# A graph layer on one core: ScalarE and SyncE wait on the gathers' own semaphores, GpSimd waits once per group, and the lists are gathered in 124, 122, 125 and 77 rows

## The reference

```
xp    = xn @ W                                   # 4 heads of 64
e     = leaky_relu(a_src[src] + a_dst[dst], 0.2)
alpha = exp(e - segment_max(e)) / segment_sum(exp(e - segment_max(e)))
gat   = relu(segment_sum(alpha * xp[src], dst))
mix   = (v + l2norm_over_channels(q2) @ (l2norm_over_nodes(k2).T @ v) / sqrt(N)) @ W_out + b_out
x     = x + gat + mix
x     = x + sum over 8 experts of w_e * (two normed hidden layers of 256 and an output layer)(layernorm(x))
```

## Time and profile before

| what | value |
|---|---|
| median of 3 runs | 4459.44 us (4455.92 to 4459.45) |
| span of the profiled execution, first to last instruction | 3169.3 us |
| own time of the profiled execution apart from its span | not given in its page |
| median less that span | 1290.1 us |
| mean granted TensorE clock | 0.893 |
| PE busy | 2799.6 us, 88% |
| DVE busy | 2292.7 us, 72% |
| ACT busy | 1531.0 us, 48% |
| POOL busy | 1491.4 us, 47% |
| gathers of L755 | 1564 |

### The profile page before, as it was taken

One profiled execution on the slowest core, in us unless ns is written; L12 is line 12 of the kernel. 1 busy time (PEld: TensorE's weight loads), 2 busy tenths in 40 slices (PEclk: granted clock), 3 DMA queues, 4 the chain that ended last, 5 costly groups with the idle time before them and its releaser, 6 DMA issues. The chain is left out here.

```text
span 3169.3 us, 61855 instructions
## 1 busy us (share of the span) xinstructions
PE 2799.6 (88%) x18584; PEld 2138.8 (67%) x18584; DVE 2292.7 (72%) x6615; ACT 1531.0 (48%) x4018; POOL 1491.4 (47%) x1580
## 2 busy tenths in 40 slices
PE   7777787888788998889888888879999999999999
PEld 6566676666667877777766777766666666666665
DVE  7587787878788787877888888885766665656633
ACT  3354465555555666656655655653333333333332
POOL 0777777777777777777777777720000000000000
PEclk9787787888778898889887887889999999999999
DMA  9544444444445555555544444433011010101000
GB/s 307 147 120 124 121 126 121 124 122 128 118 117 132 138 141 135 141 135 136 131 124 129 122 125 124 125 99 111 10 38 36 12 35 12 35 12 35 12 12 12
DMA packets 208686, 315.91 MB, mean 100 GB/s; under 512 B 84449, under 2 KB 142818, under 8 KB 208226
## 3 DMA queue, kind: packets, MB, share of 16 engines
q0 software_dynamic: 75360, 212.42, 25.9%
q1 hardware_dynamic: 125250, 92.39, 9.7%
q10 hardware_dynamic: 7744, 7.15, 0.7%
HBM read 279.46 MB, written 26.86 MB: 97 GB/s over the span
## 5 line engine op out<-in xcount | busy, mean ns | idle before, releaser
L755 POOL DMA_INDIRECT xg<-edge_table,idx x1564 | 1486.2, 950 | 523.0 <-issue 491.4
L1059 PE MATMUL ps_y<-y,hotw 128*128 128x260 f32 x3512 | 859.0, 407 | 69.9 <-issue 68.0
L1059 PEld LDWEIGHTS ps_y<-y,hotw 128*128 128x128 f32 x3512 | 689.9, 203 | 217.2 <-issue 81.6
L1809 DVE SCALAR_TENSOR_TENSOR xg<-ps_ye,wts,xg 128x256 f32<-128x256 f32 x392 | 189.7, 484 | 401.6 <-PE ps_ye L1599 401.4
L911 ACT ACTIVATE y<-xg,w 128x65 f32 x1756 | 463.3, 337 | 7.1
L1291 DVE TENSOR_TENSOR y<-xg,ps_v 128x780 f32<-128x780 f32 x439 | 417.0, 960 | 8.9 <-DVE ps_v L1284 0.5
L1642 ACT ACTIVATE tables<-ps_h,bnb,bns 128x448 f32<-128x448 f32 x224 | 162.3, 724 | 494.2 <-PE ps_h L1589 494.2
L970 ACT CAST hotw<-hot 128x512 f32<-128x512 bf16 x439 | 266.5, 622 | 246.4 <-PE ps_y L1059 246.0
L1599 PE MATMUL ps_ye<-wo,xg 128*128 128x256 f32 x1568 | 354.2, 383 | 0.2 <-DVE xg L1809 0.2
L1589 PE MATMUL ps_h<-xg,w 128*128 128x448 f32 x896 | 347.5, 541 | 1.0 <-issue 0.5
L1589 PE MATMUL ps_h<-tables,w 128*128 128x448 f32 x896 | 345.9, 539 | 0.0
(11 more groups left out here) (283 smaller groups left out, 3155.6 us busy)
## 6 DMA issues: line engine op xcount, KB each, us to landing
xg<-edge_table,idx POOLq DMA_INDIRECT x1564
mix_rows<-kk SPq DMA_DIRECT2D x49, 257.0 KB
xg<-mix_rows SPq DMA_DIRECT2D x7, 1799.0 KB, 8.4
xb<-in_xt SPq DMA_DIRECT2D x50, 128.0 KB
xnk<-in_x SPq DMA_DIRECT2D x50, 128.0 KB
x<-in_x SPq DMA_DIRECT2D x7, 896.0 KB, 11.4
xt<-in_xt SPq DMA_DIRECT2D x7, 896.0 KB, 13.4
xb<-in_xt SPq DMA_DIRECT2D x24, 256.0 KB
```

Of the source, the lines that this page charges most:

```text
L755: pool.indirect_dma_start(xg[:, q * OCT + u, j, :], None, dr["table"], bass.IndirectOffsetOnAxis(ap=idx[o % IDX][:, c:c + 1], axis=0)).the ...
L1059: mm = pe.matmul(ps_y[v % 2][:, 0:RW], hotw[v % 2][:, j, :], y[v % 2][:, j, :], start=(j == 0), stop=(j == CH - 1))
L1809: dve.scalar_tensor_tensor(yb[q][:, j, :], ps_y[j % 2][:, 0:D], wts[q][:, j, e:e + 1], yb[q][:, j, :], ALU.mult, ALU.add).then_inc(S["expe ...
```

## The change

Three things change.

The semaphore `landed` is gone. ACT and SP wait on `got[0]` and `got[1]` themselves. The count for each is made by `words` for both parities, so `K.need` becomes two tables, with three DVE operations each in place of one, and ACT reads four values per step in place of two.

GpSimd no longer waits ahead of a group's fourth gather for the group before. It waits ahead of a group's first gather for the last group but one, which is the last with the same semaphore.

The four list gathers take 124, 122, 125 and 77 rows (`LIST`, starting at `LAT`), and all that handles the lists follows.

```diff
-VT = NVT // P + 1
+LIST = (124, 122, 125, 77)
+LAT = (0, 124, 246, 371)
+VT = len(LIST)
...
-        rows = [min(P, NVT - t * P) for t in range(VT)]
+        rows = LIST
...
                 def words():
-                    link(dve.tensor_scalar(K.need[:], grp[0:1, :], 1.0, float(ONE), ALU.add, ALU.add))
+                    for k in range(2):
+                        link(dve.tensor_scalar(slot_i[:], grp[0:1, :], 2.0 - k, None, ALU.add))
+                        link(dve.tensor_scalar(slot_i[:], slot_i[:], 1, None, ALU.arith_shift_right))
+                        link(dve.tensor_scalar(K.need[k][:], slot_i[:], 1.0, 16.0 * CH, ALU.max, ALU.mult))
...
+                        if not first or u >= 2:
+                            pool.wait_ge(got[u % 2], 16 * CH * ((o * OCT + u) // 2))
                         for j in range(CH):
-                            if j == CH - 1 and not (first and u == 0):
-                                pool.wait_ge(got[(u - 1) % 2], o * (16 * CH * OCT // 2) + 16 * CH * ((u - 1) // 2 + 1))
-                                pool.sem_inc(landed, 1)
                             c = u * CH + j
...
-                    sp.wait_ge(landed, ONE + (o - IDX + 1) * OCT)
+                    for k in range(2):
+                        sp.wait_ge(got[k], 16 * CH * (o - IDX + 1) * OCT // 2)
...
-                        need.append(act.value_load(K.need[0:1, bass.ds(n(SV) + v, 1)], min_val=ONE + 1, max_val=ONE + NGP))
+                        need.append([act.value_load(K.need[k][0:1, bass.ds(n(SV) + v, 1)], min_val=16 * CH, max_val=16 * CH * NGP) for k in range(2)])
...
-                            act.wait_ge(landed, need[v > 0])
+                            for k in range(2):
+                                act.wait_ge(got[k], need[v > 0][k])
```

More of the change, by code:

```diff
@@ L234, in _ @@
                             sp.wait_ge(rows_in[t], 16)
-                            sp.dma_start(dr["dst"][t * P:t * P + rows[t], :], xrows[0:rows[t], t, 0:GE]).then_inc(stored, 16)
+                            sp.dma_start(dr["dst"][LAT[t]:LAT[t] + rows[t], :], xrows[0:rows[t], t, 0:GE]).then_inc(stored, 16)
                 for k in range(IDX):
@@ L288, in turn_groups @@
                     for t in range(VT):
-                        pe.transpose(ps_g[0:rows[t], t * P:(t + 1) * P], grp[:, t * P:t * P + rows[t]], ident).then_inc(gt_d, 1)
+                        pe.transpose(ps_g[0:rows[t], t * P:(t + 1) * P], grp[:, LAT[t]:LAT[t] + rows[t]], ident).then_inc(gt_d, 1)
                 def turn_lists(t):
@@ L386, in lists_out @@
                     act.wait_ge(last_t, t + 1)
-                    act.copy(K.last[:, t * GE:t * GE + r * CH].rearrange("p (v j) -> p j v", j=CH),
+                    act.copy(K.last[:, LAT[t] * CH:LAT[t] * CH + r * CH].rearrange("p (v j) -> p j v", j=CH),
                              ps_l[:, 0:GE].rearrange("p (j v) -> p j v", j=CH)[:, :, 0:r]).then_inc(lastc_d, 1)
@@ L510, in spreads @@
                     r = rows[t]
-                    at = slice(t * GE, t * GE + r * CH)
+                    at = slice(LAT[t] * CH, LAT[t] * CH + r * CH)
                     dve.wait_ge(rel_t, t + 1)
@@ L514, in spreads @@
                                       ps_r[:].rearrange("p (j v) -> p j v", j=CH)[:, :, 0:r],
-                                      bc(base[:, t * P:t * P + r], 1, CH), ALU.subtract).then_inc(rel_d, 1)
+                                      bc(base[:, LAT[t]:LAT[t] + r], 1, CH), ALU.subtract).then_inc(rel_d, 1)
                 def centre(i):
@@ L619 @@
     score_capped weights_done values_copied q_turned q_squared q_fourth mix_products mix_copied hot_widened y_done_act max_joined tail_first tail_second
-    tail_third pair_parts max_shifted max_leaky y_done y_summed acc_scaled acc_done asrc_packed iota_set weights_spread fold_spread groups_landed
+    tail_third pair_parts max_shifted max_leaky y_done y_summed acc_scaled acc_done asrc_packed iota_set weights_spread fold_spread
     k_products k_biased k_squared k_less k_scales k_normed k_sums_done k_sums_added k_columns_added one_set k_rooted kv_products kv_done root_bounded
@@ L684, in attend @@
          vo_d, qt_d, q2_d, q4_d, mix_d, mixc_d, hotw_d, ya_d, msum_d, tp1_d, tp2_d, tp3_d, pp_d, z1_d, lk1_d,
-         y_d, py_d, sc_d, acc_d, as_d, iota_d, wv_d, fov_d, landed,
+         y_d, py_d, sc_d, acc_d, as_d, iota_d, wv_d, fov_d,
          k_d, kb_d, k2_d, kr1_d, kr_d, kn_d, ka_d, kas_d, col_d, one_d, root_d, kv_d, kvs_d, lim_d, rec_d, kv1_d,
@@ L759, in _ @@
                     octet(o % 2, o, o == 0)
-                pool.wait_ge(got[(NG - 1) % 2], 16 * CH * ((NG + 1) // 2))
-                pool.sem_inc(landed, 1)
+                for k in range(2):
+                    pool.wait_ge(got[k], 16 * CH * ((NG + 1 - k) // 2))
                 for c in K.exp.values():
@@ L1848, in graph_layer @@
             K.blk, K.slot = ml.sb("blk", [1, NVT // 4], I32), ml.sb("slot", [1, NVT // 4], I32)
-            K.need = ml.sb("need", [1, NVT], I32)
+            K.need = [ml.sb(f"need{k}", [1, NVT], I32) for k in range(2)]
             K.freed = ml.sb("freed", [1, NGP // PACE], I32)
```

## The result

The changed kernel takes 4475.86 us (median of 20 runs, 4463.61 to 4491.41), the kernel before on the same chip 4459.52 us (20 runs, 4445.55 to 4480.04). The ratio is 1.0033, with a 95% interval of 1.0021 to 1.0046: slower by 16.3 us between the medians and by 15 us by the ratio, where the forecast was 6.4 us faster. 4475.86 lies outside the range of 4438 to 4467.

A forecast was written before the change was run, and what follows sets the result against it. GpSimd's pace of one gather every 1.25 us was taken to bound the edge loop up to about 1680 us, the consumer after. Terms -10 + 2.0 + 1.6 = -6.4 us gave 4459.4 - 6.4 = 4453.0 us, range 4438 to 4467.

The forecast's parts named there:

- The lists: In `prepare`, ahead of the edge loop: uneven list gathers lengthen the transfers by 1.6 us, with 0 and 3.3 as ends.
- by the rule the sum would be 1.7 us higher: List gathers: if the largest divisor up to 16 sets the engines (4, 2, 5, 11), the sum rises 1.7 us.
- `words`: +2.0 us: Ahead of `rstd(6)`: five more DVE operations delay the last rows, barrier and first gather by 2.0 us, in full.
- The moved wait: -10 us: GpSimd in the edge loop: waiting at a group's first gather saves 10 us on the path, bounds 8 and 11.
- the direct waits: ACT and SP waiting on the DMA semaphores themselves: 0 us, with -2 us as the bound.
- The tail: End of the edge loop: last gather near 2076 us, the last step's copies 10 to 14 us after it.
- More value loads: 0: ACT, two more loads per step: hidden behind queued products and a wait for PE, 0 us, upper bound +3 us.
- neither rival on them: GpSimd's pauses after 112 gathers: they shrink, 4442 down to 4430 us, chance 0.16; or multiply, 4480 us or 4507, chance 0.08.
- the new wait still binds: Rival, GpSimd: landings slow with more gathers under way, GpSimd keeps its 11 us, time 4463 us; chance 0.08.
- The gain is given back: Rival, edge loop: the consumer cannot use earlier gathers, only some 4 of 10 us arrive, 4459 or 4461 us; chance 0.18.
- 1290.1 us: Difference between profile span and timed median: assumed to lie outside the span and to be untouched by the change.

The follow-up runs named there:

- e11: The changed kernel with even lists and the `words` chain moved behind the last reciprocal root and spread, against the kernel before, quick session: 3159.30 us, ratio 0.9968.
- e9: The changed kernel as it is, run again in a quick session, against the kernel before: 3171.95 us, ratio 1.0010.
- e2: The kernel before with only the lists changed to 124, 122, 125 and 77 rows, slow session: 4481.73 us, ratio 1.0041 to the kernel before.
- e18: The changed kernel with even lists and GpSimd's wait back at the fourth gather, quick session: 3162.65 us, ratio 0.9983 to the kernel before.
- e13: The changed kernel with even lists and GpSimd's wait back at the fourth gather, slow session: 4508.54 us, ratio 0.9988 to the kernel before.
- e14: The kernel before with only the four uneven lists, in a later slow session: 4521.63 us, ratio 1.0023 to the kernel before.
- e1: The kernel before, unchanged, under another name, slow session: 4476.69 us, ratio 1.0025 to the kernel before.

## Why the prediction was wrong

**The lists, which is the step that failed.** The prediction put +1.6 us, with 3.3 as upper end, from the bytes on the fullest engine. The first gather of sixteen profiles by lists and by `words` (us):

| | one operation in `words` | six |
|---|---|---|
| even lists | 80.1, 80.5, 80.6, 80.8, 80.9, 81.1, 82.0 | 82.0, 82.7, 82.9, 83.5 |
| uneven lists | 92.6, 93.3 | 92.2, 92.7, 93.0 |

By the means, uneven lists alone cost 92.9 - 80.9 = 12 us, beside the six operations 92.6 - 82.8 = 10 us. The bound of 3.3 us was no bound. It took the fullest engine to get some 40 rows more, without a working for the 40, and counted the rows once, for the gathers. It left out that the gathers' packets multiply (1088 for 288), that SP stores the same rows again, over 12.7 us in place of 6.5, and that x stands in SP's queue behind them. By the rule of the Trainium skill (DMA: Bandwidth & Descriptors) named above, and if one engine took part in all four stores, it would get 31 + 61 + 25 + 7 = 124 rows in place of 28, which at the prediction's 24 GB/s is an estimate of 8 us. So "by the rule the sum would be 1.7 us higher" did not follow from the rule for the stores. DVE was already waiting 2.44 us for x; that was the place to ask what queues there.

**`words`: +2.0 us.** Right with even lists, 82.8 - 80.9 = 1.9 us, though 82.0 us occurs with one operation and with six, and `e11` takes most of it back. With uneven lists nothing of them is seen, 92.6 us against 92.9. Why is not shown: ACT still waits 2.22 us for the reciprocal in `e9` and 0.69 us in `e2`, and the 8.16 us for x lie ahead of `words`, where they can hide nothing behind them. The sum added two terms that together cost no more than the larger one.

**The moved wait: -10 us.** The amount was right in a quick session by luck, the cause was not: the loop fell from 2059.1 to 2049.2 us, but `e18` shows that all but 2 us of it comes without the move. I had put the direct waits at 0 with -2 as bound. The waits of up to 1.70 us, read as a cost that every execution pays, shrink with the wait in its old place too; whether the direct waits do that or the profile of before was a long one stays open. The tail was as expected in its distance, not in its time (2076 us was forecast): the last gather starts at 2083.4 us, and the last copies, at 2094.91 in place of 2094.39, stand 11.5 us behind it.

**More value loads: 0.** Held: the 220 loads leave that distance as it was (11.4 us before), and ACT's idle time ahead of its `asrc` copies after 1680 us stays small, 2.8 us (0.8 for a gather, 2.0 under "issue") against 3.4.

**The pauses.** 13 of some 2.4 us before and after in the quick sessions: neither rival on them came true. Nor did "the new wait still binds". "The gain is given back" named ACT's waits between 1040 and 1680 us as the danger, and PE and DVE as what takes over; in the quick sessions nothing of the kind is seen.

**What lay outside the span.** The prediction took 1290.1 us as time beside the span that the change doesn't touch, and carried the difference over. They are the slow session's loop, 3360 us in place of 2059. In it the pace of GpSimd is covered, and the gain of 10 us is not to be seen in loops that scatter by 12 us within one session and by 28 us between two runs of another (`e13`, `e14`), while the stage ahead of the loop is as exposed as ever.

So the sum of a quick session is +12 - 10 = +2, against a ratio of 1.0010, which is +3.2 us (0.3 to 6.0); the medians, 3171.95 and 3167.81, differ by 4.1. That of a slow session is +12 + 0 against +15 (9 to 21), with the caution that equal kernels differed by 11 us there (`e1`). I take the direction as shown, for two reasons: the first gather of every slow profile with uneven lists starts some 12 us later than that of the kernel before, and the four slow-session ratios with them, 1.0023, 1.0033, 1.0038 and 1.0041, lie above the two of changed kernels with even lists, 0.9988 and 0.9998. The 1.0025 of `e1`, an unchanged kernel, lies among the four, so the first reason carries more. The size, 0.33%, is no better known than the 0.25% of `e1` allows.

## What to carry to other kernels

Where the span of the profile and the timed median lie as far apart as here, 3169 and 4459 us, the profile can be of another regime, and a term read from it (who sets the pace) holds only there; terms from a stage that runs the same in both, such as a prologue, carry over. Ask of a reshaped transfer how many packets it makes, which other transfers of the same rows change with it, and what is queued behind them; and compare with row counts that are multiples of 16: here they saved 10 to 12 us. Two delays on the way to one point need not add up: look at where each is waited for.

## What was not expected of the hardware

- Four indirect gathers of 124, 122, 125 and 77 rows of 2 KB make 1088 packets and land in 11.3 us (median), of 128, 128, 128 and 64 rows 288 packets and 7.2 us. GpSimd itself is busy 1.44 us in place of 0.95 with one. Plain stores of the same row counts take 12.7 us in place of 6.5, and 6.4 us when each is cut into a multiple of 16 rows and the rest.
- One kernel takes 3163 to 3169 us in some sessions and 4460 to 4515 us in others, and the chip with number 7 had both. The difference lies in visits that run beside indirect gathers, 5.8 to 6.0 us in place of 1.9 in the mean, and half the gathered bytes do not change it.
- GpSimd pauses for 2.4 us after every 112 gathers in the changed kernel's slow profile too, 13 times, whatever idle times lie between, so it goes by the count. In the changed kernel's slow profile a pause comes nine gathers after an idle time of 6.96 us:

```profile
1668.33 0.94 POOL L759 DMA_INDIRECT xg<-edge_table,idx  x1 [6.96 <-ACT y L917]
...
1682.02 0.95 POOL L759 DMA_INDIRECT xg<-edge_table,idx  x1 [2.39 <-issue]
```
